# Second cross attention of a four-layer block: eight buffers of rounded weights, and one 384-column TensorE pass per head whose result is not read

## What is computed

```
q = (x @ Wq + bq).reshape(1, B * N, H, hd)          # 1024 queries, 16 heads of 16
k, v = ...                                          # 1024 keys and values
q, k = fq_sym(q * scale, axis=-1), fq_sym(k, axis=-1)
v = fq_sym(v, axis=2)
attn = softmax(q @ k^T)                             # 1024 x 1024 per head
attn = clip(round(attn / s), 0, 255) * s,  s = max(attn) / 255
out = (attn @ v) @ Wp + bp
```

## Time and profile before

| | |
|---|---|
| median of three runs | 1005.2 us |
| the profiled execution, its whole time | 1008.87 us |
| its span, first to last instruction | 1007.1 us |
| mean granted TensorE clock | 0.849 |
| core loop of the second cross attention | 346.3 to 536.8 us |
| granted clock within it | 0.50 from 347.6 us on |
| DMA transposes in it | 128 of 256 KB |

### The profile page before, as it was taken

The page is one execution under the profiler, slowest core; times in us unless marked ns, Lnnn a source line. Parts: engine busy times, 40 slices in busy tenths (PEclk is TensorE's granted clock), DMA queues, the critical chain, the costliest instruction groups (busy, mean ns, idle before and its releaser), DMA issues.

```text
span 1007.1 us, 17047 instructions
## 1 busy us (share of the span) xinstructions
PE 911.9 (91%) x5954; PEld 545.8 (54%) x5954; DVE 668.3 (66%) x1331; ACT 405.3 (40%) x683; POOL 343.2 (34%) x365
## 2 busy tenths in 40 slices
PE   7898899999998688889997897989899999999997
PEld 4466665443666444444455454555796658754443
DVE  4987755442569988889994969654112502589998
ACT  3343331310027787788881635631134355210000
POOL 4232203010035476777772621005104557200002
PEclk9997877999999755555557998979899999789999
DMA  9200003000000099999993016056314234000001
GB/s 297 30 1 1 1 1 100 0 1 0 1 1 1 6 180 178 182 180 189 191 184 82 1 37 174 13 138 155 120 48 142 69 95 135 2 0 0 0 0 42
DMA packets 189451, 74.96 MB, mean 74 GB/s; under 512 B 152737, under 2 KB 187196, under 8 KB 189388
## 3 DMA queue, kind: packets, MB, share of 16 engines
q1 hardware_dynamic: 187852, 69.93, 32.5%
q0 software_dynamic: 1536, 4.20, 1.3%
HBM read 33.20 MB, written 7.34 MB: 40 GB/s over the span
## 4 chain that ended last, share of the span: by engine, by line
PE 59%; DVE 16%; DMA 11%; POOL 5%; issue 4%; ACT 4%; SPq 0%; DVEq 0%; ACTq 0%; POOLq 0%
DMA hT<-hT 10%; PE psum L1986 10%; PE psum L446 6%; POOL hT L1048 4%; PE psum L483 3%; PE psum L1543 3%; PE psum L596 2%; PE psum L612 2%; PE psum L450 2%; PE psum L1232 2%; PE psum L426 2%; PE psum L1825 2%; PE psum L337 2%; PE psum L604 1%; PE psum L1786 1%
## 5 line engine op out<-in xcount | busy, mean ns | idle before, releaser
L1112 DVE TENSOR_REDUCE am<-psum 128x1024 f32 (+1 forms) x128 | 154.9, 1222 | 20.1 <-PE psum L958 16.7
L1021 ACT ACTIVATE arena<-psum,am 128x1024 f32<-128x1024 f32 x128 | 142.5, 1113 | 31.0 <-POOL hT L1048 19.8
L1048 POOL TENSOR_SCALAR hT<-arena 128x1024 f16<-128x1024 f32 x128 | 133.9, 1046 | 61.8 <-DMA hT<-hT 32.4
L958 PE MATMUL psum<-arena 96*128 96x512 bf16 x256 | 130.1, 612 | 16.6 <-ACT arena L1021 12.4
L320 POOL TENSOR_TENSOR rstd<-ve,neg_half 128x1 f32<-128x1 f32 x64 | 39.3, 618 | 221.6 <-DVE ve L310 221.3
L1986 PE MATMUL psum<-arena,cT 128*128 x512 | 112.8, 384 | 1.5 <-DVE xn L2044 1.5
L2044 DVE SCALAR_TENSOR_TENSOR xn<-psum,small,xn 128x256 f32<-128x256 f32 x248 | 103.9, 477 | 3.3 <-PE psum L1986 0.2
L1986 PEld LDWEIGHTS psum<-arena,cT 128*128 128x128 f16 x512 | 50.5, 99 | 63.5 <-issue 2.2
L969 PEld LDWEIGHTS psum<-arena,hT 128*128 128x128 f16 x512 | 51.5, 113 | 50.5 <-DMA hT<-hT 24.5
L969 PE MATMUL psum<-arena,hT 128*128 128x16 f16 x512 | 58.6, 185 | 9.1 <-DMA hT<-hT 8.6
L970 PEld LDWEIGHTS psum<-arena,m 128*128 128x128 f16 x512 | 49.4, 114 | 29.9 <-issue 29.6
(11 more groups left out here) (342 smaller groups left out, 1817.2 us busy)
## 6 DMA issues: line engine op xcount, KB each, us to landing
hT<-in_L_ffn_expert_masks SPq DMA_DIRECT2D x32, 256.0 KB, 2.9
arena<-in_L_ffn_w_gate SPq DMA_DIRECT2D x2, 1408.0 KB
arena<-in_L_ffn_w_up SPq DMA_DIRECT2D x2, 1408.0 KB
arena<-in_L_ffn_w_down SPq DMA_DIRECT2D x2, 1408.0 KB
moe_in<-xT SPq DMA_DIRECT2D x2, 1024.0 KB, 6.8
hT<-hT SPq DMA_TRANSPOSE x128, 3.3
hT<-moe_in SPq DMA_DIRECT2D x4, 512.0 KB, 5.5
moe_out<-arena SPq DMA_DIRECT2D x16, 128.0 KB, 1.7
```

What stands on the lines that cost most here:

```text
L958: mm = pe.matmul(psum[:, score_banks(c), :][:, g, :], QT[0:SPLIT, c % H, bass.ds(row_tile(j, c) * P, P)], KT[0:SPLIT, c % H, g * HALF:(g + ...
L1021: act.activation(PE1[:, c % 2, :], psum[:, score_banks(c), :].rearrange("p a b -> p (a b)"), ACT.Exp, bias=am[:, bass.ds(n, 1)], accum_out ...
L1048: pool.tensor_scalar(Y1[:, n % Y_SLOTS, :], PE1[:, n % 2, :], 255.0, 1024.0, ALU.mult, ALU.add)\
L1112: dve.tensor_reduce(am[:, bass.ds(n, 1)], psum[:, score_banks(c), :], AX.XY, ALU.max, negate=True)\
```

## The change

`Y_SLOTS` goes from four to eight. The first four buffers lie where they lay (two in each of two rows of `hT`); two more lie in the arena behind `V1_pairs` and two at its start, where the operand stacks of the projection lay, which have been read by then. POOL so waits for the transpose of head n-8 in place of n-4.

In each step that has outputs, PE now first does one matmul of 96 rows by 384 columns, keys against keys of that head, into columns 128 to 511 of the output bank. Nothing reads them. It stands behind the wait for the landed transpose and behind the wait for the copied bank, and ahead of the twelve output matmuls.

```diff
@@ -235,11 +235,12 @@
+        y_homes = [hT[:, 4, :], hT[:, 5, :], a.tile([T]), Arena(arena).tile([T])]
...
-        PT_SLOTS, Y_SLOTS = 8, 4
+        PT_SLOTS, Y_SLOTS = 8, 8
...
-        Y1 = hT[:, 4:6, :].rearrange("p a n -> p (a n)").bitcast(FP16).rearrange("p (s n) -> p s n", s=Y_SLOTS)
+        Y1 = [home.bitcast(FP16)[:, i * T:(i + 1) * T] for home in y_homes for i in range(2)]
@@ -830,6 +831,7 @@
         LAG_V = 7
+        W_COLS = 384
@@ -965,6 +967,8 @@
                     o = out_bank(c)[:, at:at + HD]
+                    pe.matmul(out_bank(c)[:, P:P + W_COLS], KT[0:SPLIT, c % H, 0:P], KT[0:SPLIT, c % H, 0:W_COLS],
+                              start=True, stop=True)
                     for k in range(0, NB, 2):
@@ -1045,7 +1049,7 @@
-                pool.tensor_scalar(Y1[:, n % Y_SLOTS, :], PE1[:, n % 2, :], 255.0, 1024.0, ALU.mult, ALU.add)\
+                pool.tensor_scalar(Y1[n % Y_SLOTS], PE1[:, n % 2, :], 255.0, 1024.0, ALU.mult, ALU.add)\
@@ -1146,7 +1150,7 @@
-                sp.dma_start_transpose(PT1[:, n % PT_SLOTS, :, :], Y1[:, n % Y_SLOTS, :]).then_inc(turned(n % H), 16)
+                sp.dma_start_transpose(PT1[:, n % PT_SLOTS, :, :], Y1[n % Y_SLOTS]).then_inc(turned(n % H), 16)
```

## The result

The changed kernel takes 1014.7 us (median of 12 runs, 1010.3 to 1017.6), the kernel before 1006.0 us in the runs beside it (12 runs, 1000.1 to 1016.7). The ratio is 1.0073 with a 95% interval of 1.0048 to 1.0099: slower by about 7 us, or 0.5 to 1.0%. The ratio and its interval use the fast runs alone, so they need not equal the quotient of the two medians, which lie 8.7 us apart. The forecast was 1014.1 us, +8.9.

The account below looks back on a forecast made before the run. The prediction took SP's issue of transposes to bound the loop, and PE once the pass is added. Its terms, 9.87 - 2.32 + 0.32 + 1.0 = +8.9 us, put on 1005.2 gave 1014.1 us, range 1002 to 1018 us.

Parts of the forecast that it names:

- SP's issue bounds the loop before: In the loop, SP's issuing of transposes sets the pace: 1.386 us apart in the quiet stretch, 1.437 us on average.
- The pass takes PE past SP: In each loop step with outputs, 0.320 us more makes PE's step 1.513 us, above SP's 1.437: +9.87 us over 120 steps.
- The load of the pass is hidden: The pass's stationary load, 0.105 us, lies beside the matmul ahead of it and costs 0.
- rival 3: The pass's load is exposed, 0.105 us a head: +21.6 us, 1026.8 us; chance 0.06 together with longer stalls.
- The queue at the end goes, -2.32 us: At the loop's end, last pair to last landing takes 7.95 us instead of 10.27, with no queue at POOL and SP.
- Stalls behind fetches, +1.0 us: In the loop, nine instruction fetches delay landings, up to 0.4 us lost each, 0 to 3.6 us in all; +1.0 taken.
- slack of 2.6 us: In the loop, a landing is wanted 10.6 us behind its pair and comes after 7.95, leaving 2.6 us.
- The last head's outputs have a pass ahead of them, +0.32 us: Behind the last landing, the last head's outputs wait for one more pass: +0.32 us.
- The eight buffers bring 0 behind a PE that bounds: In the loop, buffers are worth 0 if PE bounds, otherwise about 2 us, bounded by 0 and 6.5.
- rival 1: The clock rises in the loop, SP bounds again and buffers bring 2 us: net -2.5, 1002.7 us; chance 0.20.
- The clock stays at 0.50: In the loop, TensorE's granted clock stays low despite the pass; low clock with PE bound, chance 0.62, 1010 to 1018 us.
- Rival 2, absorbed: The pass is absorbed in the loop, step at most 1.44 us, no change: 1004 to 1007 us; chance 0.12.

Follow-up runs that it names:

- pass_only: The changed kernel with four buffers instead of eight, keeping the 384-column pass; ratio to the kernel before 1.0068 (1.0032 to 1.0104), loop 196.21 us.
- buffers_only: The changed kernel without the pass, keeping eight buffers; ratio to the kernel before 0.9992 (0.9958 to 1.0026), loop 190.40 us.
- rows_128: The changed kernel with its pass over 128 rows (constant fp16 block against fp16 values) instead of 96; ratio to the kernel before 1.0015, loop 190.29 us.
- its control: The 128-row pass kernel with the same fp16 operands cut to 96 rows; ratio to the kernel before 1.0056 (1.0022 to 1.0089), loop 195.83 us.

## Why the prediction held, step by step

- *SP's issue bounds the loop before.* Shown. Buffers, a pass of 192 or 256 columns, and the full clock all leave it at 190 to 191 us.
- *The pass takes PE past SP.* Shown. The step was 1.494 us, not 1.513. The 0.02 us lies ahead of the outputs: a pair starts 0.81 us before what follows it (482.26 to 483.07), where in the steps of before it was up to 0.83, and the sum took 0.853. Over 120 steps this is 2.3 us of the 9.87. The steps moved the last pair back by (530.05 - 350.82) - (525.95 - 354.26) = 7.54 us.
- *The load of the pass is hidden.* Shown, rival 3 falls: the pass starts 0.80 us behind the pair's start (480.77 to 481.57), and the small matmuls and the next pair follow without a gap.
- *The queue at the end goes, -2.32 us.* It was -1.48: 538.84 - 530.05 = 8.79 us from the last pair to the last landing, not 7.95. The last but one transpose took 2.16 us to issue beside a code fetch, and the last waited for it. The chain that ended last shows it:

```profile
533.84 1.05 POOL arena L1052
534.89 0.68 SPq L1153
...
535.66 3.18 DMA hT<-arena
```

- *Stalls behind fetches, +1.0 us.* There were none: in the 120 steps PE has no gap. Of L970's 7.0 us of waits for landings 3.1 are its load's, beside a running matmul, and the rest lies behind the last pair. But the slack of 2.6 us was mis-sized. It took each landing to come 7.95 us behind its pair, and until about 480 us SP was behind, so that landings came up to 11.2 us behind. That of head 20 came at 381.49 us, and its pass started at 381.54, 0.05 us later. That the stalls were 0 is narrow luck; only from about 480 us on was the slack near 3 us.
- *The last head's outputs have a pass ahead of them, +0.32 us.* Shown: the transposes on PE behind the loop begin 541.01 - 538.84 = 2.17 us after the last landing, where before it was 538.08 - 536.22 = 1.86.
- *The eight buffers bring 0 behind a PE that bounds.* Shown by pass_only. The 2 us that rival 1 gave them where SP bounds was wrong: the loops of buffers_only and rows_128 are no shorter than before, where two profiles differ by 0.4 us. The excess of 6.5 us over SP's floor is longer issues beside code fetches, which more buffers don't shorten.
- *The clock stays at 0.50.* It did, and the argument that the prediction took from the rows, that the passes over 96 rows are not the kind that brought it back elsewhere, is now borne out by the pair of rows_128 and its control. Rival 1 fell on both counts: with 96 rows the clock does not rise, and with 128, where it does, there is nothing to gain.
- *Rival 2, absorbed.* It is true of a pass of up to 256 columns.

The loop grew by 6.1 us: 7.54 for the steps, -1.48 at the end. The prediction had 8.55 for the same. Outside the loop the two profiled spans differ in both directions. The changed kernel's loop began 3.4 us earlier, at 342.83 us, and its rest took 474.8 us in place of 470.9. The clock came back only at 552 us, 13.5 us behind the last landing, where before it was at 542, 5.9 us behind. Matched instruction by instruction, 3.4 of the 3.9 us arise in the first 16 us behind the last landing, so the low clock is their likely cause:

```profile
545.90:549.30 3.40, 3.40 (x9) 1.98 (x8) 0.91 (x2) 0.00 (x0) 0.00 (x0) 0.50 0.00 0
549.30:552.30 3.00, 3.00 (x8) 1.37 (x6) 1.00 (x4) 0.00 (x0) 0.57 (x1) 0.50 0.00 0
552.30:555.70 3.40, 3.40 (x15) 2.21 (x14) 3.22 (x13) 0.00 (x0) 1.30 (x2) 1.00 0.00 0
```

In the second profile of the changed kernel the clock came back 10.3 us behind the last landing, and that part took 470.6 us. In pass_only it came back 6.5 us behind. Whether the pass delays the clock's return is not shown. So the agreement of 1014.1 with 1014.7 to half a microsecond is luck; the terms were good to about 2 us (the steps 2.3 too many, the end 0.8 too few, the stalls 1.0 too many). The 7.3 us by the ratio against 6.1 in the loop and 0.3 behind it leaves about 1 us that its interval (4.8 to 10.0 us) doesn't let one place.

## What to carry to other kernels

Ask who sets the pace by changing one engine's work alone: PE was busy for 97% of a stretch and yet had room for 256 columns a head, since the queue that issues the transposes was the bound, with no busy share of its own in the page. Waits for a buffer that vanish when buffers are added prove nothing, unless the pace behind them changes. And before work is added to raise TensorE's clock, look whether anything waits for TensorE at the low one.

## What the runs showed that was not expected

- A pass of 384 columns over 128 rows brought the clock back to 1.00 for two thirds of the loop. Over 96 rows of the same operands it stayed at 0.50, and so it did with 768 columns of keys over 96 rows, while PE was busy without a gap for most of the loop.
- An issue of a 256 KB transpose took SP 1.288 us at the median while the next block was always ready, and 1.232 us when it came after a wait.
- A body of 48 heads with one more matmul per head than before was not fetched again for its second pass. With two more it was, with five to six fetches of 16 KB in 50 us, and PE once stood still for 4.4 us. Three matmuls less per head undid it.
